# Images sent in groups of 1, 2, 3, 4, 4 and 1 with ten residual places, and VectorE's short dependent operations ordered one by one

## The reference

```python
x = x + _L0_conv_ref(_ln_c(x), ...)       # layernorm over channels, then:
    # q, k, v = W_qkv @ rmsnorm(x), 4 heads of 32
    # q = softmax(q, over the 32 dims);  k = softmax(k, over the 1024 tokens)
    # out = rmsnorm(W_out @ ((k @ v.T) @ q) + b_out)
t = _to_tokens(x)
t = t + _L0_ffn_ref(_ln_t(t), ...)        # layernorm over channels of each token, then:
    # probs = softmax(xf @ gate_w + gate_b)             # 8 experts
    # top2_vals, top2_idx = top_k(probs, 2)
    # out = sum over the 2 of  val * (gelu(xf @ W1[e] + b1[e]) @ W2[e] + b2[e])
```

## Time and profile before

| | us |
|---|---|
| median of 3 runs (lowest, highest) | 804.19 (803.08, 806.5) |
| the profiled execution | 799.15 |
| its span, first to last instruction | 797.3 |
| busy: TensorE, its weight load | 677.3 (85%), 570.4 (72%) |
| busy: VectorE | 602.9 (76%) |
| busy: ScalarE | 562.9 (71%) |
| busy: GpSimd | 490.7 (62%) |

### The profile page before, as it was taken

One profiled execution on the slowest core, in us unless ns is written; L12 is line 12 of the kernel. 1 busy time (PEld: TensorE's weight loads), 2 busy tenths in 40 slices (PEclk: granted clock), 3 DMA queues, 4 the chain that ended last, 5 costly groups with the idle time before them and its releaser, 6 DMA issues. The chain is left out here.

```text
span 797.3 us, 16397 instructions
## 1 busy us (share of the span) xinstructions
PE 677.3 (85%) x4270; PEld 570.4 (72%) x4270; DVE 602.9 (76%) x2244; ACT 562.9 (71%) x1440; POOL 490.7 (62%) x504
## 2 busy tenths in 40 slices
PE   5866458999987978999979978987999599899997
PEld 3544336888776848886868667876986488799896
DVE  6898888876986797979988879967798875743333
ACT  2632225776976868888978788887887587677654
POOL 1007444443377777777777777777777777777151
PEclk9985787999998999999999999999999889999999
DMA  7701235776876685987787597778885779956922
GB/s 176 225 20 51 81 98 182 209 256 204 258 234 212 219 265 173 309 270 221 257 277 242 177 316 215 243 250 288 244 287 179 237 213 308 302 178 174 330 63 70
DMA packets 118564, 169.70 MB, mean 213 GB/s; under 512 B 20145, under 2 KB 81097, under 8 KB 118473
## 3 DMA queue, kind: packets, MB, share of 16 engines
q1 hardware_dynamic: 102056, 136.95, 54.9%
q0 software_dynamic: 15360, 31.49, 12.9%
q10 hardware_dynamic: 1056, 0.22, 0.2%
HBM read 110.24 MB, written 60.96 MB: 215 GB/s over the span
## 5 line engine op out<-in xcount | busy, mean ns | idle before, releaser
L766 POOL DMA_INDIRECT rows_in<-xf_tok,row_of x240 | 251.1, 1046 | 173.0 <-DVE row_of L1256 99.5
L781 POOL DMA_INDIRECT y_rows<-rows_out,row_back x240 | 237.2, 989 | 117.7 <-issue 71.6
L1479 PE MATMUL y_ps<-wb,hid 128*128 128x128 f32 x1664 | 222.1, 281 | 28.5 <-ACT hid L883 27.1
L1479 PEld LDWEIGHTS y_ps<-wb,hid 128*128 128x128 f32 x1664 | 207.7, 195 | 46.3 <-ACT hid L883 37.8
L883 ACT ACTIVATE hid<-h_ps,wb 128x256 f32<-128x256 f32 x416 | 173.8, 476 | 73.0 <-PE h_ps L1469 52.9
L1469 PE MATMUL h_ps<-xt,wb 128*128 128x256 f32 x704 | 186.3, 391 | 7.8 <-DMA wb<-experts 4.5
L1469 PEld LDWEIGHTS h_ps<-xt,wb 128*128 128x128 f32 x704 | 124.8, 196 | 23.7 <-DMA wb<-experts 6.5
L1389 PE MATMUL ab<-wqkv_t,x_sb 128*128 128x392 f32 x256 | 108.7, 548 | 18.7 <-ACT qkv L821 14.6
L1310 DVE TENSOR_TENSOR yb<-y_ps,wb 128x256 f32<-128x256 f32 x176 | 71.7, 418 | 57.2 <-PE y_ps L1479 47.6
L869 ACT ACTIVATE y_rows<-y_rows,share 128x128 f32<-128x128 f32 x240 | 83.0, 411 | 32.3 <-DMA y_rows<-rows_out,row_back 32.1
L821 ACT ACTIVATE qkv<-ab,root 128x392 f32<-128x392 f32 x128 | 72.3, 590 | 36.5 <-PE ab L1389 22.7
(11 more groups left out here) (197 smaller groups left out, 970.0 us busy)
## 6 DMA issues: line engine op xcount, KB each, us to landing
wb<-experts SPq DMA_DIRECT2D x176, 321.0 KB
xb<-rows_in SPq DMA_DIRECT2D x176, 128.0 KB
rows_out<-yb SPq DMA_DIRECT2D x176, 128.0 KB
rows_in<-zeros SPq DMA_DIRECT2D x85, 128.0 KB, 2.2
x_sb<-in_x_dram SPq DMA_DIRECT2D x16, 512.0 KB, 6.2
out_dram<-out_sb SPq DMA_DIRECT2D x32, 256.0 KB, 3.8
rows_in<-xf_tok,row_of POOLq DMA_INDIRECT x240
y_rows<-rows_out,row_back POOLq DMA_INDIRECT x240, 4.1
```

What stands on the lines that cost most here:

```text
L766: pool.indirect_dma_start(out=rows_in[p % IN_BUFS], out_offset=bass.IndirectOffsetOnAxis(ap=row_of[:, n % X1_RING, k, t:t + 1], axis=0), i ...
L781: pool.indirect_dma_start(out=y_rows[:, r, k, :], out_offset=None, in_=rows_out[p % OUT_BUFS][0:BLOCKS[p] * ROWS, :], in_offset=bass.Indir ...
L1479: last = pe.matmul(y_ps[:, b % Y_BUFS, i * P:(i + 1) * P], hid[:, b % 2, k, i * P:(i + 1) * P], wb[:, r, HIDDEN + k * CH:HIDDEN + (k + 1) ...
```

## The change

**Groups.** The images are sent in groups of 1, 2, 3, 4, 4 and 1: blocks 15, 23, 31, 39, 39 and 15, which are 162. Six plans are made. Buffers of the plan grow with the largest group. **Places.** `X1_RING` is ten.

**VectorE's steps.** `parts()` makes a step for each single instruction, or for a few that don't depend on each other; the program waits at the start of the dependent instruction, and `then` is gone. So other steps may stand between two links of a chain. `x1` is done in halves. `k_part` becomes one reduction over a permuted view.

**The planner.** A VectorE step that needs a step of VectorE counts as ready only a delay after it (0.12), and a free engine may hold out up to `AHEAD` = 0.15 for a more urgent step, with a `short` one put before it if that fits. TensorE, ScalarE, POOL and SP do the same for an image and for a block as before; only their order differs.

```diff
-GROUPS = (2,) * 7 + (1,)
+GROUPS = (1, 2, 3, 4, 4, 1)
...
-X1_RING, XF_RING, BACK_RING, YG_RING, OUT_RING = 8, 3, 3, 16, 4
+X1_RING, XF_RING, BACK_RING, YG_RING, OUT_RING = 10, 3, 3, 16, 4
...
+ROOT, SIZE, AHEAD = 10, 11, 0.15
...
+    def parts(engine, name, lengths, after, more=0.12):
+
+        for i, length in enumerate(lengths):
+            part = name + (i,)
+            step(engine, part, length, [last_part[name]] if i else after, more)
+            last_part[name] = part
...
-        step("DVE", a("k_part"), 1.4, [a("qkv7")] + chain("k_part") + chain("KT"), 0.15)
+        step("DVE", a("k_part"), 1.14, [a("qkv7")] + chain("KT"), 0.12)
...
-        step("DVE", a("root_s"), 2.2, [a("square2")] + chain("norm2"), 0.05)
-        step("DVE", a("x1"), 1.14, [a("norm2")], 0.1)
...
+        parts("DVE", a("root_s"), (0.085,) * SIZE, [a("square2")] + chain("norm2"))
+        for h in range(2):
+            step("DVE", a(f"x1_{h}"), 0.6, [a(f"norm{h + 1}")] + ([a("x1_0")] if h else []), 0.1)
...
-            step("DVE", of("add", n, h), 1.35, [("weigh", n, h * HT + HT - 1)] + before, 0.1)
+            parts("DVE", of("add", n, h), (0.6, 0.6), [("weigh", n, h * HT + HT - 1)] + before)
...
-            found = [name for name in ready[e] if ready_at[name] <= now and (steps[name][4] is None or open_banks)]
+            found = [name for name in ready[e] if ready_at[name] <= now + AHEAD and (steps[name][4] is None or open_banks)]
...
             name = max(found, key=lambda x: (urgency[x], str(x)))
+            if ready_at[name] > now:
+                short = [x for x in found if ready_at[x] <= now and now + steps[x][1] <= ready_at[name] + AHEAD]
+                if not short:
+                    continue
+                name = max(short, key=lambda x: (urgency[x], str(x)))
...
-                in_order = steps[f][0] == e and (e != "SP" or f[0] == name[0])
+                in_order = steps[f][0] == e and (e in ("PE", "ACT", "POOL") or f[0] == name[0] and e == "SP")
...
-                    then(dve.tensor_tensor(four.rearrange("p (t c) -> p t c", c=P), k[:, 0:4, :], k[:, 4:8, :], ALU.max),
-                         s_k_part, n * 3 + 1)
-                    then(dve.tensor_tensor(two, four[:, 0:2 * P], four[:, 2 * P:4 * P], ALU.max), s_k_part, n * 3 + 2)
                     wait(dve, s_kt_mm, n)
-                    dve.tensor_tensor(k_part[:, :], two[:, 0:P], two[:, P:2 * P], ALU.max).then_inc(s_k_part, 1)
+                    dve.tensor_reduce(k_part[:, :], k.rearrange("p t c -> p c t"), X_AXIS, ALU.max).then_inc(s_k_part, 1)
...
-                then(dve.tensor_tensor(t, y, y, ALU.mult), step, base + 6)
-                then(dve.tensor_tensor(t, t, v, ALU.mult), step, base + 7)
...
+                if i > 0:
+                    dve.wait_ge(step, base + i)
...
+                if i == 5:
+                    last = dve.tensor_tensor(t, y, y, ALU.mult)
+                if i == 6:
+                    last = dve.tensor_tensor(t, t, v, ALU.mult)
...
+                last.then_inc(step, 1)
```

More of the change, by code:

```diff
@@ L158, in attention @@
             before = [a(f"norm{h - 1}")] if h else [a("root_s")] + old("logits", 2)
-            step("DVE", a(f"norm{h}"), 0.27 * len(F_TILES[h]) + 0.1, before, 0.1)
-        step("DVE", a("root_s"), 2.2, [a("square2")] + chain("norm2"), 0.05)
-        step("DVE", a("x1"), 1.14, [a("norm2")], 0.1)
[L162 to L166, removed]
+            step("DVE", a(f"norm{h}"), 0.26 * len(F_TILES[h]) + 0.12, before, 0.1)
+        parts("DVE", a("root_s"), (0.085,) * SIZE, [a("square2")] + chain("norm2"))
+        for h in range(2):
+            step("DVE", a(f"x1_{h}"), 0.6, [a(f"norm{h + 1}")] + ([a("x1_0")] if h else []), 0.1)
+            parts("DVE", a(f"bn2_{h}"), (0.39, 0.39), [a(f"x1_{h}")] + ([a("bn2_0")] if h else chain("stats2")), 0.1)
+        parts("DVE", a("stats2"), (0.25, 0.25, 0.09), [a("bn2_1")] + old("xf1", 2) + old("pair_r", 3))
+        step("DVE", a("logits0"), 0.14, [a("norm2"), a("gx")] + chain("choose"))
+        parts("DVE", a("logits"), (0.14, 0.14), [a("logits0"), a("pair_r")])
+        parts("DVE", a("scores"), (0.14, 0.14), [a("logits")])
+        parts("DVE", a("first"), (0.14, 0.14, 0.14), [a("scores")] + ([("table", group_of(n) - 1)] if n in FIRST[1:] else []))
         step("ACT", a("exp"), 0.2, [a("scores")], 0.1, table="exp")
@@ L275, in lay_out @@
     steps["load", 0] = e, length, more, after + [("spare", 0)], bank, done, table
+    for name, (engine, length, more, after, bank, done, table) in steps.items():
+        steps[name] = engine, length, more, [last_part.get(a, a) for a in after], bank, [last_part.get(a, a) for a in done or ()], table
     return arrange(steps)
@@ L943, in r2, with attention @@
                 return root[:, (n + 1) % PAIR_RING, 1, :]
-            def attention(what, n):
+            def attention(what, n, i):
                 mine = qkv[:, n % QKV_RING, :, :]
@@ L1031, in attention @@
                         ALU.mult).then_inc(s_y, 1)
-                if what == "x1":
-                    dve.wait_ge(s_y, n * 3 + 3)
+                for h in [h for h in range(2) if what == f"x1_{h}"]:
+                    half = slice(h * HT, (h + 1) * HT)
+                    dve.wait_ge(s_y, n * 3 + h + 2)
                     dve.wait_ge(s_x_tok, n * 2 + 2)
-                    dve.tensor_tensor(x1, x_tok[:, n % TOK_RING, :, :], x1, ALU.add).then_inc(s_x1, 1)
+                    dve.tensor_tensor(x1[:, half, :], x_tok[:, n % TOK_RING, half, :], x1[:, half, :], ALU.add).then_inc(s_x1, 1)
@@ L1059, in attention @@
                 if what == "scores":
-                    scores(n)
+                    scores(n, i)
+                if what == "first":
+                    first_choice(n, i)
                 for h in [h for h in range(2) if what == f"xf{h}"]:
@@ L1191, in _ @@
+                if i == 2:
+                    wait(dve, s_pair, ROOT * n)
+                    dve.tensor_tensor(spread[:, (n + 1) % PAIR_RING, 1, :], st2[:, 1, :], st2[:, 2, :], ALU.add).then_inc(s_st2, 1)
             ranks = rank[:, :].unsqueeze(1).broadcast_to((P, TILES, EXPERTS))
             logits, below, exps, work, rest, again = (gate[:, i, :, :] for i in range(6))
-            top, total, second, best, spare = (gate_stat[:, i, :] for i in range(5))
+            top, total, second = (gate_stat[:, i, :] for i in range(3))
@@ new lines, in make_plan @@
+                if step == 0:
+                    dve.wait_ge(s_place, PLACE * (sent_before(last) + 1))
+                    wait(dve, s_back, p)
+                    if p >= PLAN_RING:
+                        dve.wait_ge(s_zeroed, 16 * EXPERTS * (p - PLAN_RING + 1))
+                        dve.wait_ge(s_bt, BLOCK0[p - PLAN_RING + 1])
+                    dve.tensor_copy(plan[:, p % PLAN_RING, 2 * MAX_BLOCKS:], ends)
+                    dve.tensor_tensor(counts, ends, region[:, :], ALU.subtract).then_inc(s_plan, 1)
+                    return
@@ new lines, in make_plan @@
+                if step == 7:
+                    dve.tensor_reduce(tab_s[:, 1, 0:blocks], tab_b[:, 1, 0:blocks, :], X_AXIS, ALU.add)
+                    dve.tensor_scalar(plan[:, p % PLAN_RING, MAX_BLOCKS:MAX_BLOCKS + blocks], tab_s[:, 0, 0:blocks],
+                                      float(EXPERTS - 1), float(P), ALU.min, ALU.mult).then_inc(s_plan, 1)
+                if step == 8:
+                    dve.tensor_tensor(plan[:, p % PLAN_RING, 0:blocks], tab_s[:, 1, 0:blocks], block_row[:, 0:blocks],
+                                      ALU.add).then_inc(s_plan, 1)
```

477 lines of the change are left out of this document (269 added, 208 removed).

## The result

The changed kernel takes 776.72 us (773.21 to 780.7, 4 runs) where the kernel before takes 804.48 (803.08 to 806.5, 4 runs): a ratio of 0.967, 95% interval 0.963 to 0.971. The forecast was 797. The profiled execution took 775.42 us with a span of 773.7, 23.6 less than before. One trace further down, that of places_only, is of a slow execution: 835.4 us, where that kernel's other four took 822.75 to 825.48.

The account below looks back on a forecast made before the run. GpSimd was taken as full from 211 to 742, the other engines close behind. 535 to image 13's row numbers, 137 to image 10's fetch, 103 for five fetches and 15.2 make 790.2, 7.1 saved: 797 us, range 766 to 816.

Parts of the forecast that it names:

- GpSimd was full, and the larger groups free it ahead of r: GpSimd, 528 of 531 us filled by DMAs from 211 to 742; new groups leave 426 us of DMAs ahead of r.
- r: The time of image 13's row numbers, splitting the kernel in two stretches: 594.56 before, forecast 535, between 517 and 550.
- Links 24.4, takes 9.3, adds 8.4, plans 3.1: VectorE up to r: us saved by 203 fewer dependent neighbours, 28 fewer takes, 14 fewer adds, two plans of fewer instructions.
- `k_part`, 0.4 gained: VectorE up to r: one permuted reduction, assumed as fast as an ordered one at 1.211, saves 0.4 us over 14 images.
- Waits, 15: ScalarE up to r: 15 of its 32.1 us of waiting for fetched rows go, with a third fewer fetches.
- Tail 255.2: The stretch behind r: 137 to image 10's fetch, 103 for five fetches, 15.2 to the end; 202.7 before.
- the sum by bytes: Big group's 39 blocks behind r: 31.4 MB at 300 GB/s take 105 us, ready at r + 137.
- the rivals 2.29 and 2.90: Us per block for the big group's 39 blocks: 2.29 in the faster rival (0.2), 2.90 in a slower one (0.15).
- Sum: Whole kernel: r at 535 plus 137, 103 and 15.2 gives a span of 790.2 us, 7.1 less than before.
- the first rival: All 32 us of ScalarE's waits go and blocks run at 2.29: r 517, tail 244.8, 769 us; chance 0.2.
- Ten places at nothing: Residual places, ten instead of eight: taken to cost or save nothing of their own ahead of r.
- The links buy nothing: VectorE up to r: separating dependent instructions saves nothing, so r is 559.6 and the time 821 us; chance 0.15.

Follow-up runs that it names:

- places_only: The kernel before with ten residual places and the one-instruction `k_part`, old groups and old planner: 825.17 us, 1.029 of the kernel before.
- planning_only: The changed kernel with the old groups (seven of two, one of one), ten places and finer steps kept: 809.87 us, 1.011 of the kernel before.
- planning0_only: The changed kernel with the old groups and the hold-out `AHEAD` at 0 instead of 0.15: 801.26 us, 0.998 of the kernel before.
- kfold_s14: The changed kernel with `k_part` as three maxima and image 14's whole send ordered before image 10's first fetch: 785.03 us, 0.976 of the kernel before.
- groups8: The kernel before with the new groups alone, eight places, whole VectorE steps and old planner: 831.71 us, 1.038 of the kernel before.
- groups_places: The kernel before with the new groups, ten places and the one-instruction `k_part`, without the finer steps: 795.86 us, 0.992 of the kernel before.
- kfold_no_ahead: The changed kernel with `k_part` as three maxima and the hold-out `AHEAD` at 0: 767.06 us, 0.958 of the kernel before.
- ring8: The changed kernel with eight residual places instead of ten: 821.09 us, 1.023 of the kernel before.
- links_blind: The changed kernel with `AHEAD` at 0 and a planner that takes a VectorE link to cost nothing: 823.63 us, 1.029 of the kernel before.
- no_ahead: The changed kernel with the planner's hold-out `AHEAD` at 0 instead of 0.15: 751.70 us, 0.938 of the kernel before.
- a05_s14: The changed kernel with `AHEAD` at 0.05 and image 14's whole send ordered before image 10's first fetch: 752.26 us, 0.935 of the kernel before.

## Why the prediction was right in direction and too small

By its own steps, against the changed kernel:

- *GpSimd was full, and the larger groups free it ahead of r*: right. Between its first fetch and r its waits of over 0.4 us add up to 3.5 us before and 33.4 in the change. (13 sends stand ahead of r, not 14: image 13's is counted again behind r.) With the old groups neither planning_only nor planning0_only was faster.
- *Links 24.4, takes 9.3, adds 8.4, plans 3.1*: right as a sum. With `x1` and `k_part` they were put at 44.4; with what `k_part` really costs (next) that is 34.6, and VectorE's own time fell by 35.7. The terms were not measured one by one.
- *`k_part`, 0.4 gained*: wrong. The reduction over the permuted view takes 1.916, not 1.211. It cost 14 x (1.83 - 1.16) = 9.4, within the bounds of the text; 9.8 less than was put down. Undoing it (kfold_s14) gains nothing in r: 47 more links stand together, own time falls by 3.2 only, and VectorE waits 8.7 more.
- *Waits, 15*: **this is the step that failed.** It read ScalarE's waits for fetched rows and halved them; ahead of r they did fall, by 14 (23.3 to 9.2). But r is the sum of VectorE's own time and VectorE's waits, and these waits fell by 31.5, twice what was put down: 19.2 of it for ScalarE (squares alone 19.5 to 4.6), 6.3 for TensorE, 5.8 for DMAs. groups8 and groups_places, with the old planner and whole steps, show that the groups carry this fall. That it comes from the 28 blocks and three fetched images fewer which TensorE and ScalarE have ahead of r is argued, not shown: with the same groups the squares' waits are back at 20.9 in kfold_no_ahead, where VectorE needs less time of its own. The step looked at the wrong engine's waits. That r is only 7.6 off is partly luck: the 9.8 of `k_part` hide more than half of the 16.5 that this step lacks.
- *Tail 255.2*: 246.3, the other half of the miss. First product of the large group at 561.9, r + 34.5 (35.6 forecast). Its 39 blocks took 2.38 each (561.92 to 654.69), where the sum by bytes gave about 2.6 and the rivals 2.29 and 2.90. The DMA pace was 305 GB/s up to the last product (300 forecast), and from 557 to image 10's first fetch 31.5 MB moved (31.4 forecast); that fetch came at r + 132.2 instead of r + 137. The five fetches took 102.8 (103). From the last fetch's end to the end of the span 11.3 instead of 15.2; why is open.
- *Sum*: r 7.6 early, tail 8.9 short, 773.7 instead of 790.2. That is near the first rival: its tail (244.8) and some 40% of its way in r (from 535 to 517). In medians the forecast of 797 is 20 high, since the changed kernel's median lies only 1.3 above its profiled execution and not 5.0 as before.
- *Ten places at nothing*: wrong, though the sum for ten places does not show it. Without them the change is 44 us slower (ring8): the tail's cover for the last group needs image 14's send before image 10's fetches.
- *The links buy nothing* (second rival): the runs decide against it. Own time follows the count of neighbours, 507.0 at 732, 490.3 at 589, 439.1 at 225, all with the new groups. links_blind fits less well: 493.3 at 674, 3.0 more than the change for 85 neighbours more, with six takes and two adds fewer ahead of r. The Trainium skill's rule that the prediction set beside this rival ("VectorE: DVE Perf Modes", section "The DRAIN you can't avoid") has an exception that the prediction left out: the section adds that a next operation which is not held starts earlier. The independent rows that follow each other after 0.07 to 0.08 agree with it.

The whole now reads: the groups move load behind r, the places keep image 14 in time, the finer steps shorten VectorE, and only together do they bring more than 1%. Groups alone are at 1.038, places (with `k_part`) at 1.029, groups and places at 0.992, groups and finer steps at 1.023 (ring8), places and finer steps at 1.011, all three at 0.967. Why VectorE's waits differ from order to order (57 to 82 us at some 225 neighbours) stays open.

GpSimd's list shows the same from the other side. Leaving out places_only, its 480 DMAs took 625 to 636 us with the short gaps between them in every trace (635.6 before, 624.9 in the change). Its waits of over 0.4 us and the end behind its last fetch differ more: 163 us before, 150 in the change, 125 in no_ahead, 123 in a05_s14, 202 in groups8. What shortens VectorE thus shows in the time only as far as it also shortens these.

## What to carry to other kernels

Ask which engine is the slowest in a stretch and add up that engine's own waits, not another's; here larger groups, which move load off the others, took these from 68.6 to 45.7 by themselves. Where a planner may hold an engine for a more urgent step, keep the hold-out shorter than the delay that other work should fill: 0.15 against 0.12 kept links together that 0.10, 0.05 and 0 let other work part. And look at the last small group: whether its input is sent whole before the long run of fetches decided 19 and 23 us in two pairs of kernels with the same work.

## What the runs showed of the hardware

A maximum over eight tiles read through a permuted view took 1.916 us for 1024 elements per partition, where a reduction of as many elements in order took 1.214 and three halving maxima 1.41 together. A short VectorE instruction (0.17 us) that depends on the one right before it starts 0.20 after it; in no_ahead another instruction put between two such starts 0.07 to 0.08 after the first. Over the stretch up to r each link so filled was worth 0.12 us of VectorE's own time from groups_places to the change (143 neighbours fewer) and 0.14 from the change to no_ahead (364 fewer); links_blind shows less.
